# Four chained transformer blocks on one core: the plain attentions' value product with the roles of weights and V exchanged

## The reference, cut to what matters

```python
logits = einsum('bhqd,bhkd->bhqk', qh, kh) / sqrt(16)      # + mask * -1e9, or where(mask, -inf, ...)
attn = softmax(logits, axis=-1)
out = einsum('bhqk,bhkd->bhqd', attn, vh)                   # per head 128 x 128 by 128 x 16
out = out.transpose(0, 2, 1, 3).reshape(B, S, 256) @ wo + bo
x = layernorm(x + out)                                      # block 2; block 3 normalises ahead instead
```

## Time and profile before

| | us |
|---|---|
| median of 3 runs | 2249.19 |
| lowest and highest | 2244.71, 2249.86 |
| the profiled execution | 2250.39 |
| its span | 2248.7 |
| busy: PE, PEld | 1905.0, 1495.8 |
| busy: DVE, ACT, POOL | 1303.7, 962.4, 995.3 |

### The profile page before, as it was taken

One profiled execution on the slowest core, in us unless ns is written; L12 is line 12 of the kernel. 1 busy time (PEld: TensorE's weight loads), 2 busy tenths in 40 slices (PEclk: granted clock), 3 DMA queues, 4 the chain that ended last, 5 costly groups with the idle time before them and its releaser, 6 DMA issues.

```text
span 2248.7 us, 29935 instructions
## 1 busy us (share of the span) xinstructions
PE 1905.0 (85%) x10497; PEld 1495.8 (67%) x10497; DVE 1303.7 (58%) x2218; ACT 962.4 (43%) x2270; POOL 995.3 (44%) x1235
## 2 busy tenths in 40 slices
PE   4666667677887887887999999998988999999997
PEld 3555556454664665665877777786766787787776
DVE  5877778659568668568454563544633625535361
ACT  1111122224334334334555565454644656556562
POOL 5566666536336345345243453434433324333340
PEclk8888999677887887887999999999989999999999
DMA  7200000000200000000000200000000000000000
GB/s 211 77 5 5 5 10 5 5 1 6 80 1 5 6 1 6 6 1 6 5 1 6 80 6 6 1 6 5 1 6 5 6 6 1 20 10 1 10 1 10
DMA packets 31339, 35.61 MB, mean 16 GB/s; under 512 B 3196, under 2 KB 30040, under 8 KB 30808
## 3 DMA queue, kind: packets, MB, share of 16 engines
q1 hardware_dynamic: 31192, 33.70, 5.0%
HBM read 31.60 MB, written 2.10 MB: 15 GB/s over the span
## 4 chain that ended last, share of the span: by engine, by line
PE 58%; DVE 12%; issue 4%; POOL 3%; ACT 2%; DVEq 0%; POOLq 0%; ACTq 0%
PE ps L503 30%; PE ps L670 9%; PE ps L701 7%; PE ps L680 7%; PE ps L514 3%; DVE xn L874 2%; DVE rowmax L1010 1%; PE ps L696 1%; DVE work L1004 1%; DVE rowsum L1016 1%; POOL work L1199 1%; DVE work L1012 1%; PE ps L668 1%; DVE rowmax L1008 1%; ACT work L829 1%
## 5 line engine op out<-in xcount | busy, mean ns | idle before, releaser
L503 PE MATMUL ps<-hT,w_slot 128*128 128x256 f32 x1856 | 447.1, 394 | 21.0 <-ACT hT L744 21.0
L503 PEld LDWEIGHTS ps<-hT,w_slot 128*128 128x128 f32 x1856 | 354.0, 196 | 75.4 <-ACT hT L744 23.9
L1190 POOL TENSOR_TENSOR work<-KT,own_head 128x512 f32<-128x512 f32 x256 | 261.2, 1045 | 291.5 <-ACT KT L756 234.9
L680 PEld LDWEIGHTS ps<-ident,work 128*128 128x128 f32 x1536 | 205.1, 154 | 178.6 <-issue 110.8
L670 PE MATMUL ps<-work,QT 128*128 128x512 f32 x512 | 277.8, 625 | 24.4 <-POOL work L1190 21.1
L680 PE MATMUL ps<-ident,work 128*128 128x128 f32 x1536 | 264.3, 300 | 37.4 <-POOL work L1199 36.9
L886 DVE TENSOR_TENSOR x_all<-ps,x_all 128x512 f32<-128x512 f32 x88 | 60.7, 690 | 375.4 <-PE ps L503 273.6
L1199 POOL TENSOR_SCALAR work<-work,winv 128x128 f32<-128x128 f32 x512 | 183.1, 378 | 202.1 <-DVE winv L1029 201.5
L829 ACT ACTIVATE work<-work,rowmax 128x128 f32<-128x128 f32 x768 | 244.9, 392 | 62.7 <-DVE rowmax L1008 61.1
L701 PEld LDWEIGHTS ps<-V,work 128*128 128x128 f32 x2048 | 251.2, 192 | 5.9 <-ACT work L818 3.4
L701 PE MATMUL ps<-V,work 128*128 128x17 f32 x2048 | 248.6, 254 | 2.0 <-ACT work L818 2.0
(11 more groups left out here) (118 smaller groups left out, 3001.9 us busy)
## 6 DMA issues: line engine op xcount, KB each, us to landing
ctx_in<-in_ctx SPq DMA_DIRECT2D x32, 256.0 KB, 2.7
w_slot<-in_L_xattn_W SPq DMA_DIRECT2D x2, 1024.0 KB, 6.4
w_slot<-in_L_xattn_ff_w SPq DMA_DIRECT2D x1, 2048.0 KB, 11.4
w_slot<-in_L_xattn_ffn_w SPq DMA_DIRECT2D x2, 1024.0 KB, 9.4
w_slot<-in_L_xattn_w SPq DMA_DIRECT2D x2, 1024.0 KB, 9.1
out<-x_all SPq DMA_DIRECT2D x8, 256.0 KB, 2.3
x_all<-in_x SPq DMA_DIRECT2D x1, 1536.0 KB, 11.7
pad<-in_mask_Bx1x1xS_fk SPq DMA_DIRECT2D x1, 1024.0 KB, 6.8
```

What stands on the lines that cost most here:

```text
L503: mm = pe.matmul(dst, lhsT(k), rhs(k), start=(k == 0), stop=(k == chunks - 1))
L680: mm = pe.transpose(bank(2 + u % 2)[:, tok(h)], prob[u % NP][:, tok(h)], ident[:, :])
L1190: pool.tensor_tensor(KB[u % NK].rearrange("p (h k) -> p h k", h=HU), keys, own_head[:, half * HU:(half + 1) * HU].unsqueeze(2).broadcast_t ...
```

## The change

In the plain attentions the turned weights become the moving operand. Stationary is one head's V, laid out as the quantised attention does it: `V` becomes `[P, G, 8, 4, 16]`, a pair of heads with zeros between, and 32 columns of it hold one head in its upper or lower half. Head `h` of four writes the strip of PSUM rows `32h` to `32h + 31`; two units (`e` = 0 and 1) add up in one strip, one head each. The same is done with a block of ones, `ones_pair`, so that each row of PSUM also gets its head's sums. So `values_pair` handles two units at once: 2 (V, ones) x 2 (`e`) x 4 (strips) = 16 matmuls of 128 columns, issued at every second step. Which heads a unit holds changes to fit (`own_head[:, e:HC:2]`).

The result is transposed, a **quarter** (128 features x 128 tokens) per pair. VectorE takes the reciprocal of 128 x 128 sums (into the room of `O`) and multiplies straight into `OT`. `ot` and ScalarE's copy of it disappear for the plain attentions (`direct`), and `y` waits for all four quarters. `live` moves from the outputs to the adding of `y` in block 3's second attention. `PTF` has four buffers, two of them taken from `prob`, which keeps six (`NPF`). The quantised attention's `Vzb` now lies in the room of `V`, so V is filled with zeros once more at layer 2's first `v` of each stream. The waits follow.

```diff
@@ parts of the program @@
-        V = two("V", [P, G, H, DH + 1])
+        V = two("V", [P, G, H // 2, 4, DH])
+        ones_pair = sb("ones_pair", [P, 4, DH])
-        oinv = rowinv
+        oinv = [[o[:, n // 2, n % 2 * P:(n % 2 + 1) * P] for n in range(U // 2)] for o in O]
+        NPF = NP - 2
+        PTF = PT + prob[NPF:NP]
@@ TensorE @@
                     elif piece == "y":
-                        if "direct" in arg:
+                        if n["plain"]:
+                            pe.wait_ge(s["quarter_out"], U // 2 * (phase("plain", layer, g, n["mix"] - 1, st) + 1))
+                        elif "direct" in arg:
...
-                    else:
-                        for h in range(HU):
-                            hh = u % UJ * HU + h
-                            mm = pe.matmul(bank(4 + j)[:, hh * width:(hh + 1) * width], PT[u % 2][:, tok(h)], V[st][:, j, hh, :],
-                                           start=True, stop=True)
...
+                def values_pair(u):
+
+                    j, m = u // UJ, u % UJ // 2
+                    pe.wait_ge(s["PT_ready"], U * ap + u + 2)
...
+                    if U // 2 * pp + u // 2 >= C:
+
+                        pe.wait_ge(s["quarter_out"], U // 2 * pp + u // 2 + 1 - C)
+                    for summed in range(2):
+                        cols = slice((2 * j + summed) * S, (2 * j + summed + 1) * S)
+                        for e in range(2):
+                            for h in range(HU):
+                                own = ones_pair[:, 2 * e:2 * e + 2, :] if summed else V[st][:, j, m * HU + h, 2 * e:2 * e + 2, :]
+                                mm = pe.matmul(bank(4 + m)[h * 32:(h + 1) * 32, cols], own, PTF[(u + e) % 4][:, tok(h)],
+                                               start=(e == 0), stop=(e == 1))
+                    mm.then_inc(s["o_ps"], 2)
...
                     if 0 <= i - lag - 1 < U:
-                        values(i - lag - 1)
+                        if quant:
+                            values(i - lag - 1)
+                        elif (i - lag - 1) % 2:
+                            values_pair(i - lag - 2)
@@ ScalarE @@
-                        act.wait_ge(s["o_ps"], U * ap + u - 1)
+                        act.wait_ge(s["o_ps"], U * ap + u + 1 - (2 if quant else 4))
...
-                            act.activation(PT[u % 2], bank(2 + u % 2), ACT.Copy).then_inc(s["PT_ready"], 1)
+                            act.activation(PTF[u % 4], bank(2 + u % 2), ACT.Copy).then_inc(s["PT_ready"], 1)
@@ VectorE @@
+                        if layer == 2 and n["att"] == 0 and g == 0:
+
+                            dve.memset(V[st][:, :, :, :, :], 0.0).then_inc(s["V_zeroed"], 1)
+                            dve.wait_ge(s["V_zeroed"], st + 1)
...
+                def outputs(quarter):
+
+                    j, m = quarter // C, quarter % C
+                    nth = U // 2 * phase("plain", layer, g, mix, st) + quarter + 1
+                    sums_at = (2 * j + 1) * S
+                    dve.wait_ge(s["o_ps"], U * ap + 2 * (quarter + 1))
+                    dve.reciprocal(oinv[st][quarter], bank(4 + m)[:, sums_at:sums_at + S]).then_inc(s["oinv_ready"], 1)
                     dve.wait_ge(s["oinv_ready"], nth)
...
+                    dve.tensor_tensor(OT[st][:, m, tok(j)], bank(4 + m)[:, sums_at - S:sums_at], oinv[st][quarter], ALU.mult)                        .then_inc(s["quarter_out"], 1)
...
-                    if 0 <= u < U and u % UJ == UJ - 1:
-                        outputs(u // UJ)
+                    if quant and 0 <= u < U and u % UJ == UJ - 1:
+                        quant_outputs(u // UJ)
+                    if not quant and 0 <= u < U and u % 2:
+                        outputs(u // 2)
```

More of the change, by code:

```diff
@@ L86, in events_of @@
         ev.append("turned")
-    if kind == "att" and "quant" in arg:
-        ev.append("qatt")
+    if kind == "att":
+        ev.append("qatt" if "quant" in arg else "plain")
     if kind == "ffn" and arg["act"] == "geglu":
@@ L95, in events_of @@
     return ev
-KINDS = ["ctx", "stage", "norm", "tin", "bias", "local", "att", "qatt", "mix", "out", "ffn", "geglu", "hid", "yadd", "post", "turned"]
+KINDS = ["ctx", "plain", "stage", "norm", "tin", "bias", "local", "att", "qatt", "mix", "out", "ffn", "geglu", "hid", "yadd", "post", "turned"]
 PER_PASS = {k: [sum(events_of(*s).count(k) for s in layer) for layer in STEPS] for k in KINDS}
@@ L102 @@
 PER_PASS["att_phase"] = [ST * n for n in PER_PASS["att"]]
+PER_PASS["plain_phase"] = [ST * n for n in PER_PASS["plain"]]
 PER_PASS["qatt_phase"] = [ST * n for n in PER_PASS["qatt"]]
@@ L234, in program @@
         xc = [b[:, :, :, :].rearrange("p a c t -> p (a c t)").bitcast(FP32).rearrange("p (g d) -> p g d", g=G) for b in QKb]
-        Vzb = two("Vzb", [P, G, H // 2, 4, DH], BF16)
+        Vzb = [v.rearrange("p g a x d -> p (g a x d)")[:, 0:G * D].bitcast(BF16).rearrange("p (g a x d) -> p g a x d", g=G, x=4, d=DH)
+               for v in V]
         hid = sb("hid", [P, FC, T])
@@ L644, in emit_mix @@
                 mp = phase("mix", layer, g, mix, st)
-                width = DH + 1
+                pp = None if quant else phase("plain", layer, g, mix, st)
                 lag = ATT_LAG[quant]
@@ L703, in values @@
-                    mm.then_inc(s["o_ps"], 1)
+                    m = u % UJ // 2
+                    for n in range(4):
+                        for x in range(2):
+                            pair, e = u % UJ * 2 + x, n % 2
+                            at = pair % 4 * 32
+                            rhs = below[:, :].broadcast_to([P, S]) if n < 2 else PTb[u % 2][:, tok(2 * x + e)]
+                            mm = pe.matmul(bank(4 + j)[at:at + 32, m * S:(m + 1) * S], Vzb[st][:, j, pair, 2 * e:2 * e + 2, :], rhs,
+                                           start=(n == 0), stop=(n == 3))
@@ L825, in step @@
                         else:
-                            src = prob[i % NP] if "mask" in arg else bank(i % 2)
+                            src = prob[i % NPF] if "mask" in arg else bank(i % 2)
                             for h in range(HU):
                                 at = i * HU + h
-                                ex = act.activation(prob[i % NP][:, tok(h)], src[:, tok(h)], ACT.Exp, bias=shifts[:, at:at + 1])
+                                ex = act.activation(prob[i % NPF][:, tok(h)], src[:, tok(h)], ACT.Exp, bias=shifts[:, at:at + 1])
                             ex.then_inc(s["exp_ready"], 1)
@@ L1172, in spread @@
                 def spread(u):
-                    j, m, half = u // UJ, u % UJ // 2, u % 2
+                    j, m, e = u // UJ, u % UJ // 2, u % 2
                     if u == 0 and layer == 1 and mix == 0 and st == 0 and g == 0:
@@ L1230, in _ @@
             pool.memset(below[:, :], -255.0)
+            pool.memset(ones_pair[:, 0:4:3, :], 1.0)
+            pool.memset(ones_pair[:, 1:3, :], 0.0)
             for st in range(ST):
-                pool.memset(Vzb[st][:, :, :, :, :], 0.0)
-            for st in range(ST):
-                pool.memset(V[st][:, :, :, :], 1.0).then_inc(s["consts_ready"], 1)
+                pool.memset(V[st][:, :, :, :, :], 0.0).then_inc(s["consts_ready"], 1)
             pool.wait_ge(s["consts_ready"], ST)
```

65 lines of the change are left out of this document (26 added, 39 removed), and 2 rows, old and new, of the table STEPS.

## The result

| | before | changed |
|---|---|---|
| median of the runs | 2249.34 us | 2226.11 us (2224.8 to 2227.51) |
| ratio to before | | 0.9901, 95% interval 0.9884 to 0.9919 |
| profiled execution | 2250.4 us | 2225.41 us |
| its span | 2248.7 us | 2223.7 us |

A forecast was written before the change was run, and what follows sets the result against it. TensorE was taken to bound the plain attentions. Per phase, values +1.60, turn of O -0.44 and waits +2.04 give 3.2 us; 32 phases add 102 to the profiled 2250.4: 2352 us, range 2275 to 2440.

The forecast's parts named there:

- The step that failed: Value product on TensorE: only two float32 strips overlap, 0.112 us per matmul, +0.40 us a pair, +51 us in all.
- rival B: Value product: all four strips run abreast, 1.18 us a pair, 2243 us in all, faster than before; chance 0.10.
- The turn of O: On TensorE: four matmuls, 0.44 us a phase, go away; -14 us over 32 phases.
- VectorE's quarter: Reciprocal 0.95 us and product 0.28 us on VectorE, +3.6 us a phase, hidden except ahead of the scale of `xn`.
- The replay of the phase: A phase's start followed row by row: `tin` at T+13.6 instead of T+12.46, TensorE's waits up 2.04 us a phase.
- The wait for `xn`: TensorE waits about 1.6 us at `tin` in 32 places, as VectorE's first quarter stands ahead of the scale of `xn`.
- The wait for the exponentials of unit 2: A new TensorE wait of 0.85 us ahead of turn 2, as these exponentials come no sooner than before.
- The clock: Granted clock near 0.97 from 1090 us on; +33 us if a third of the phases lost some 3 us each.
- A: The forecast itself: two strips abreast and `xn` late behind VectorE's quarter, 2352 us; chance 0.68.

The follow-up runs named there:

- strip_runs4: The changed kernel with loops over strips and units swapped, so four passes in a row go to one strip: 2234.29 us, ratio 0.994.
- strip_runs6: The changed kernel with six passes in a row to each strip, then the last two of each: 2300.5 us.
- strip_runs8: The changed kernel with the strip as outermost loop, so all eight passes of a strip stand in a row: 2377.36 us, ratio 1.0574.
- before_no_turn: The kernel before the change, without the turn of O, its copy and its waits in the plain attentions: 2229.01 us, ratio 0.9913.

## Why the prediction was wrong

**The step that failed** is the one on the strips: "In the new stream the two passes of one head follow each other **in the same strip**, and only the second can run beside the next head's first." From it came 0.112 us per matmul, 1.79 for the section, 2.19 a pair and +51 us. The trace shows 0.81 from first to last start: eight slots of 0.109, four strips in each, so the next head's first pass starts 7 ns behind this head's first and does not wait for its second. The section costs 1.01 up to the next group, entering 0.09 (turn to strips 0.53, not 0.44, in the places without a wait), leaving 0.10 (1175.41 to 1176.37, 0.96 for 0.86): 1.20 a pair, rival B's price of 1.18. Against 1.79 before that is -0.59, times 128: **-76 us**. `strip_runs4` refuted the reason itself. `strip_runs6` and `strip_runs8` show where something like it begins: six passes in a row make each strip wait for the one before it, eight run two strips at a time, and that last costs 151 us.

The prediction had both readings on the table. The Trainium skill, page "TensorE: Matmul & The Clock Gate", Part 3, gives a strict order of start and end, and I took my bf16 rows, which never put two passes of a strip side by side, for compatible with it. For passes in different column strips the runs differ: in `strip_runs8` a V pass starts at 1171.36 and ones passes that stand ahead of it at 1171.46, 1171.57 and 1171.68. The measurement decides. Whether matmuls of different strips also end out of order isn't shown: the trace's ends are modelled, and the signal hangs on the last matmul of all.

**The turn of O:** -14 for the instructions; alone it measured -20. The term left out what lies around them: 0.17 us a phase of slower neighbours and handover, by `before_no_turn`.

**VectorE's quarter** came as priced: reciprocal 0.956 us (0.95 forecast), product 0.292 (0.28). Its added busy time, 80 instead of 114 us, is smaller mainly because `xn` fell from 86.1 to 57.7 us.

**The replay of the phase** had its steps right and two numbers off. The wait for `xn` is there: 1.61 us (forecast about 1.6), 40 us more in all, but in 24 of the 32 places and not in all. That its size fits is in part luck: `xn` is ready 1.4 us sooner than forecast, and TensorE, with shorter strips and an earlier start of them, comes free for `tin` about as much sooner (near T+10.5, where the forecast's sum gives T+12.0). The wait for the exponentials of unit 2 is 0.22 us, not 0.85. I had held that these are "not sooner now"; but `y` starts at T+1.83 instead of T+2.32, the sum follows it, and the exponentials begin at T+6.06 instead of T+6.64. And the two `xn` took 1.24 us instead of 1.40. So `tin` comes at T+12.17, 1.43 us before the forecast (T+13.6) and 0.98 before rival B's T+13.15: the strips start 0.4 us sooner and take 1.2 less, of which VectorE takes 0.5 back, since a shift and its maxima (L1036, L1040) hold it until T+9.59, 0.6 us past the section's end. Before it was at T+12.46: TensorE has 0.44 + 2.69 - 1.20 = 1.93 us less ahead of it, `tin` comes 0.29 sooner, and waits and handovers take the difference.

**The sum.** By the starts of TensorE's instructions the strips give -76, and the turn of O by its instructions -14. The profiled times differ by -25.0, so +65 is left for waits; this is a remainder, not a term that was measured by itself. 56 us of it are idle in the profile's waits, 40 of them for `xn`. With the turn at the -20 of its own run the remainder is +71. So 9 to 15 us lie in shorter pauses or a slower pace behind waits, and where exactly isn't shown. Rival B's 2243 had the same terms with waits of 2.6 a phase (+83) instead of 2.0.

**The clock** stayed at 0.97 as forecast; behind the 1.61 us wait the next 4 us (1178.60 to 1182.60) show 1.00. The +33 us held ready for lost clock weren't needed.

**The range** ended at 2275, since B had a chance of 0.10. What stood for A was an argument on how strips take passes, with no row behind it; four abreast with any order of passes deserved as much.

## What to carry to other kernels

- How parallel units share one stream (strips, queues, banks) is a term with a sign of its own: where no row shows the very pattern, split the chance evenly between serial and parallel instead of arguing for one.
- An operand that comes late for two reasons (its place in the row, and a neighbour that slows it) gives up little when one is mended: some 10 us each here, 43 together. Mend both before calling either useless.
- A phase's start replayed row by row found that `tin` would wait before the run did, though its size fitted in part by luck; what the replay missed was the rows in which an engine *waits* before, since these move as soon as their releaser does.

## What the runs showed of the hardware

- Column strips in float32 overlap fully: 32 instructions of 128 columns in 0.81 us, 25 ns each, against 0.109 us for one that stands alone. Runs of up to four passes per strip keep that (0.845 us), runs of six take 1.53, of eight 2.19. If a strip holds one running and three waiting passes, the four orders need 8, 8, 14 and 20 slots, so 7, 7, 13 and 19 steps of 0.109 us from first to last start (0.76, 0.76, 1.42 and 2.07). The measured values lie 0.05 to 0.12 us above, and in `strip_runs6` and `strip_runs8` the first pass of each strip, which takes 0.13, explains this; what holds the passes was not seen.
- VectorE's scale of `xn` (128x256, SBUF to SBUF) takes 0.73 us for two with POOL idle, and 2.06 beside two key products of POOL's (1177.82 to 1179.91, 1.04 and 1.09 us, where one alone takes 1.04). Each of the two scales ends 0.15 us behind the key product that it meets. In the changed kernel POOL ends at 1177.97 and the two, begun at 1177.20, take 1.24: they end 0.47 behind POOL. It is VectorE that is held up, and POOL loses 0.05 us at most. The Trainium skill, page "SBUF — State Buffer", section "Who interferes with whom", calls the shared port pair an exclusive lock; the trace agrees.
- A reciprocal on VectorE costs by its elements: 0.203 us for 8 (out of SBUF), 0.253 for 16 and 0.956 for 128 (both out of PSUM), a straight line of 6.3 ns an element; the product beside it takes 0.292 for 128.
